# One kernel of windowed attention, layer norm, recurrent gates and a second norm: the softmax division moved into the layout of the values product, with two round trips through DRAM, new places for several transfers and new roles for the accumulator banks

## The reference

```
q, k, v = split(x @ w_in.T)                      # 16 heads of 16 features
scores = q . k / 4 + slope[head] * distance      # keys of the own and the previous block of 128
p = softmax(scores);  o = p @ v;  a = o @ w_out.T
x1 = layernorm(x + a)
for t in 16 sequences (the scan's first axis; c has one row for each of 512 tokens):
    f, i = sigmoid(x1[t] @ wf.T + c @ uf.T + bf), sigmoid(x1[t] @ wi.T + c @ ui.T + bi)
    g = tanh(x1[t] @ wc.T + c @ uc.T + bc);  c = f * c + i * g
h = tanh(x1 @ wo.T + c_final @ uo.T + bo)
out = layernorm(x1 + h)
```

## Time and profile before

| | |
|---|---|
| median of 3 runs | 994.1 us |
| the profiled execution: its own time, span of its instructions | 994.83 us, 992.7 us |
| PE busy | 911.2 us (92%), granted clock 0.955 on average |
| DVE busy | 714.1 us (72%) |
| ACT busy | 574.8 us (58%) |
| POOL busy | 409.0 us (41%) |
| DMA | 131.86 MB; the main queue's packets took 45.3% of 16 engines' span |

### The profile page before, as it was taken

The page is one execution under the profiler, slowest core; times in us unless marked ns, Lnnn a source line. Parts: engine busy times, 40 slices in busy tenths (PEclk is TensorE's granted clock), DMA queues, the critical chain, the costliest instruction groups (busy, mean ns, idle before and its releaser), DMA issues. The chain is left out here.

```text
span 992.7 us, 25986 instructions
## 1 busy us (share of the span) xinstructions
PE 911.2 (92%) x9500; PEld 749.7 (76%) x9500; DVE 714.1 (72%) x2795; ACT 574.8 (58%) x1167; POOL 409.0 (41%) x687
## 2 busy tenths in 40 slices
PE   3587889999999999999999999999999999989994
PEld 2365668888888888888888888888787876668884
DVE  7666677878787868787878787878787754337875
ACT  6044556565656565656565656565656554335786
POOL 6143343444535353535353535354444443001443
PEclk8586989999999999999999999999999989899998
DMA  7644454535454545353645454645444400131764
GB/s 265 164 124 127 131 139 132 151 122 156 124 151 128 145 134 150 123 154 125 153 128 151 128 143 137 149 131 147 133 121 138 119 23 22 44 106 46 215 204 131
DMA packets 93534, 131.86 MB, mean 133 GB/s; under 512 B 12128, under 2 KB 47584, under 8 KB 93408
## 3 DMA queue, kind: packets, MB, share of 16 engines
q1 hardware_dynamic: 93136, 129.95, 45.3%
q10 hardware_dynamic: 272, 0.26, 0.1%
HBM read 79.31 MB, written 50.33 MB: 131 GB/s over the span
## 5 line engine op out<-in xcount | busy, mean ns | idle before, releaser
L689 DVE CUSTOM_DVE_ANT_0 bank<-bank,mask 128x256 f32<-128x256 f32 (+1 forms) x1024 | 369.4, 423 | 130.7 <-PE bank L951 128.7
L448 ACT ACTIVATE Pt<-bank 128x512 f32<-128x512 f32 (+1 forms) x512 | 248.2, 536 | 193.4 <-PE bank L972 193.3
L347 POOL TENSOR_SCALAR_AFFINE_SELECT Pt<-Pt 128x512 f32<-128x512 f32 x256 | 170.4, 666 | 403.9 <-ACT Pt L448 403.9
L951 PE MATMUL bank<-Ks,Qs 59*128 59x256 f32 (+1 forms) x1024 | 148.2, 319 | 44.9 <-DVE max_q L689 31.3
L951 PEld LDWEIGHTS bank<-Ks,Qs 59*128 59x128 f32 x1024 | 107.3, 191 | 86.6 <-DVE max_q L689 42.5
L689 DVE DVE_READ_ACCUMULATOR2_ANT max_q<- 128x1 f32 x1024 | 144.9, 142 | 0.0
L349 POOL TENSOR_SCALAR_AFFINE_SELECT Pt<-Pt 128x384 f32<-128x384 f32 x256 | 144.7, 565 | 0.0
L986 PE MATMUL bank<-Pt,Vp 128*32 128x256 f32 (+1 forms) x2048 | 130.9, 377 | 0.0
L932 PE MATMUL bank<-x1T,Wg 64*128 64x512 f32 x960 | 127.9, 398 | 1.0 <-DVE o_tok L703 1.0
L932 PE MATMUL bank<-cT,Ug 64*128 64x512 f32 x960 | 125.7, 393 | 0.0
L972 PE MATMUL bank<-Qs,Ks 60*128 60x256 f32 (+1 forms) x1024 | 111.8, 271 | 0.7 <-ACT Pt L448 0.3
(11 more groups left out here) (111 smaller groups left out, 1354.7 us busy)
## 6 DMA issues: line engine op xcount, KB each, us to landing
parts_dram<-qk_parts SPq DMA_DIRECT2D x128, 256.0 KB
Qs<-parts_dram SPq DMA_DIRECT2D x128, 128.0 KB, 2.7
Ks<-parts_dram SPq DMA_DIRECT2D x128, 128.0 KB, 2.8
xt_raw<-in_xt SPq DMA_DIRECT2D x16, 512.0 KB, 4.5
Qs<-parts_dram SPq DMA_DIRECT2D x128, 64.0 KB, 2.7
Ks<-parts_dram SPq DMA_DIRECT2D x128, 64.0 KB, 2.7
x_res<-in_x SPq DMA_DIRECT2D x16, 512.0 KB, 3.9
x_dram<-y SPq DMA_DIRECT2D x16, 512.0 KB, 4.4
```

The source lines that it names most:

```text
L347: gp.affine_select(out=p4[:, :, 0:128], in_=p4[:, :, 0:128], compare_op=ALU.is_ge, fill=0.0, base=0, pattern=[[0, 4], [1, 128]], channel_m ...
L448: sc.activation(probabilities(g, 2 * pair + odd)[:, S * a:S * a + n], SC[odd][:, 0:n], ACT.Exp).then_inc(exp_done, 1)
L689: ins = ve.tensor_tensor_reduce(out=raw, in0=raw, in1=mask[:, keys], scale=1.0, scalar=MASKED, op0=ALU.add, op1=ALU.max, accum_out=max_q[: ...
L951: ins = te.matmul(MX[odd][:, 256 * (n % 2):256 * (n % 2) + 256][:, keys], Qs[rows, 2 * g + pair, n * WIN:(n + 1) * WIN], Ks[rows, 2 * g + ...
```

## The change

- In sequences 0 to 14 the division no longer goes through the token layout. After each `ctx_out` ACT waits for its own copy and sends `ctx_raw` to `ctx_dram` by a DMA from its own queue; the next `ctx_out` waits until that has landed. SP loads the 16 denominator rows into `den_q` (4 DMAs), DVE turns them (32 x 32 blocks), takes reciprocals and turns them back, SP stores them in `inv_dram` and loads them again spread over each head's 16 partitions (`inv_den`, 2 DMAs), and the contexts as `o_un` (2 DMAs). POOL multiplies the two, and ACT and DVE split `o_un` into `oT`. `ctx_transpose`, `normalise` and `o_transpose` are left for the last sequence only.
- SP: chunk 1's parts of sequence t go out in iteration t, behind the last maxima row of t - 1 and the refill of group 1, instead of at the end of iteration t - 1. The first maxima row goes ahead of the refill of group 2.
- The low part of the transposed input, `x_lo`, moves from DVE to POOL from sequence 2 on, and `x_hi` from slots 1 and 2 of the iteration before to slots 11 and 12 of the one before that.
- Banks: B0 is bank 4 and A1 bank 5 in each iteration, 6 and 7 take turns as A0 and B1. The transposes of the norm use A0 and B0, the first gates B1 and A1.
- `w_o` and `u_o` are loaded and split at the end of the attention stage, into the room of `w_in`.

```diff
+        ctx_dram = nc.dram_tensor("ctx_dram", [2, QUADS, 128, S], F32).ap()
+        inv_dram = nc.dram_tensor("inv_dram", [2, 32, S], F32).ap()
...
+            moving = PAIRS[1]
+            return (moving[t % 2], PAIRS[0][1]), (PAIRS[0][0], moving[1 - t % 2])
...
+            def load_denominators(t):
+
+                sp.wait_ge(den_cleared, 1)
+                for g in range(QUADS):
+                    wait(sp, ctx_stored[g], 16, t, 16)
+                wait(sp, inv_stored, 16, t - 1, 16)
+                rows = ctx_dram[t % 2].rearrange("g (h r) (q i) -> q (g h) r i", r=2 * D, i=128)[:, :, D, :]
+                for q in range(4):
+                    sp.dma_start(den_q[32 * q:32 * q + H, :], rows[q]).then_inc(den_in, 16)
+
+            def load_contexts(t, c):
+                for g in (2 * c, 2 * c + 1):
+                    wait(sp, ctx_stored[g], 16, t, 16)
+                wait(sp, otlo_done, 2, t - 1, c + 1)
+                rows = ctx_dram[t % 2, 2 * c:2 * c + 2].rearrange("g (h r) s -> (g h) r s", r=2 * D)[:, 0:D, :]
+                sp.dma_start(o_un[:, c, :], rows).then_inc(o_un_in[c], 16)
+
+            def store_inverses(t):
+                wait(sp, inv_turned, 1, t, 1)
+                sp.dma_start(inv_dram[t % 2].rearrange("r (q i) -> q r i", i=128), den_q[:, :]).then_inc(inv_stored, 16)
+
+            def spread_inverses(t):
+
+                wait(sp, inv_stored, 16, t, 16)
+                for c in range(KC):
+                    wait(sp, scaled_done, 2, t - 1, c + 1)
+                    rows = inv_dram[t % 2, 8 * c:8 * c + 8]
+                    sp.dma_start(inv_den[:, c, :], rows.unsqueeze(1).to_broadcast([8, D, S])).then_inc(inv_in[c], 16)
...
                 if p1: max_to_stack(t - 1, 3)
-                if now: stack(t, 1)
+                if now:
+                    stack(t, 1)
+                    if t: parts_to_dram(t, 1)
                 if p2:
                     wait(sp, y_done, 2, t - 3, 2)
                     sp.dma_start(x_res[:, :, :], x[t - 2].rearrange(tok, p=128)).then_inc(xres_in, 16)
+                if by_rows: load_contexts(t - 1, 0)
                 if real(t + 2): load_xt(t + 2)
                 if now:
+                    max_to_stack(t, 0)
                     stack(t, 2)
-                    max_to_stack(t, 0)
                     stack(t, 3)
                 if n1: parts_to_dram(t + 1, 0)
                 if now: max_to_stack(t, 1)
                 if p2:
                     wait(sp, x1_done, 4, t - 2, 4)
                     sp.dma_start(x1_dram[t - 2].rearrange(tok, p=128), y[:, :, :]).then_inc(x1_out, 16)
+                if by_rows: load_denominators(t - 1)
                 if n1: stack(t + 1, 0)
+                if by_rows: load_contexts(t - 1, 1)
                 if now: max_to_stack(t, 2)
-                if n1: parts_to_dram(t + 1, 1)
+                if by_rows:
+                    store_inverses(t - 1)
+                    spread_inverses(t - 1)
+                if t == B - 1: load_last_weights()
...
+            def x_lo(t, c):
+                wait(pool, xhi_done, 2, t, c + 1)
+                gp.tensor_tensor(xT[:, t % 2, 1, c, :], xt_raw[:, c, :], xT[:, t % 2, 0, c, :].bitcast(F32), ALU.subtract).then_inc(xlo_done, 1)
+
+            def scale_contexts(t, c):
+
+                wait(pool, o_un_in[c], 16, t, 16)
+                wait(pool, inv_in[c], 16, t, 16)
+                gp.tensor_tensor(o_un[:, c, :], o_un[:, c, :], inv_den[:, c, :], ALU.mult).then_inc(scaled_done, 1)
...
+                if p2 and t - 2 < B - 1:
+                    for c in range(KC):
+                        scale_contexts(t - 2, c)
...
+                    if real(t + 2):
+                        for c in range(KC):
+                            x_lo(t + 2, c)
...
-                wait(act, ct_ready, 4, t, g)
+                pt, pg = before(t, g)
+                if pt < B - 1:
+                    wait(act, ctx_stored[pg], 16, pt, 16)
+                else:
+                    act.wait_ge(ct_ready, g)
                 sc.activation(ctx_raw[:, :], bank[:, :], ACT.Copy).then_inc(ctx_done, 1)
-
-            def ot_hi(t, c, bank):
+                if t < B - 1:
+                    wait(act, ctx_done, 4, t, g + 1)
+                    sc.dma_start(ctx_dram[t % 2, g], ctx_raw[:, :]).then_inc(ctx_stored[g], 16)
+
+            def ot_hi(t, c):
                 if c == 0:
                     wait(act, op_ready, 2, t - 1, 2)
-                wait(act, ot_ready, 2, t, c + 1)
+                wait(act, scaled_done, 2, t, c + 1)
+                sc.activation(oT[:, 0, c, :], o_un[:, c, :], ACT.Copy).then_inc(othi_done, 1)
...
                 v_out(t, 0, A0)
+                if real(t + 2): x_hi(t + 2, 0)
                 attend(12)
                 v_out(t, 1, A1)
+                if real(t + 2): x_hi(t + 2, 1)
...
                 exps(t, 3, 3)
+                last_weights_hi()
                 c_hi(t - 2, 0)
                 c_hi(t - 2, 1)
                 layernorm(t - 1)
...
+            def turn_denominators(t):
+
+                wait(dve, den_in, 64, t, 64)
+                ve.transpose(den_t[:, :], den_q[:, :]).then_inc(den_turned, 1)
+
+            def invert_denominators(t):
+                wait(dve, den_turned, 1, t, 1)
+                own = den_t[:, :].rearrange("p (b r) -> p b r", r=32)[:, :, 0:H]
+                ve.reciprocal(own, own).then_inc(den_inverted, 1)
+
+            def turn_inverses(t):
+                wait(dve, den_inverted, 1, t, 1)
+                ve.transpose(den_q[:, :], den_t[:, :]).then_inc(inv_turned, 1)
+
+            def ot_lo(t, c):
+                wait(dve, othi_done, 2, t, c + 1)
+                minus_hi(oT[:, 1, c, :], o_un[:, c, :], oT[:, 0, c, :]).then_inc(otlo_done, 1)
...
                 attend(0)
-                if p1: normalise(t - 1, 0, A0)
+                if p3: forget(t - 3, 0)
+                attend(1)
+                if t == 0: x_lo(1, 0)
+                attend(2)
+                if t == 0: x_lo(1, 1)
                 if p2:
-                    ot_lo(t - 2, 0, B0)
-                    ot_lo(t - 2, 1, B1)
-                attend(1)
-                if n1: x_lo(t + 1, 0)
-                if p3: forget(t - 3, 0)
-                attend(2)
-                if n1: x_lo(t + 1, 1)
+                    ot_lo(t - 2, 0)
+                    ot_lo(t - 2, 1)
...
+                if p1: turn_denominators(t - 1)
                 if n1: qk_lo(t + 1, 3, B1)
-                if p1: normalise(t - 1, 3, A0)
-                if p2:
-                    x1_lo(t - 2, 0, B0)
-                    x1_lo(t - 2, 1, B1)
+                if p1: invert_denominators(t - 1)
+                if p2: x1_lo(t - 2, 0, A0)
+                if p1: turn_inverses(t - 1)
+                if p2: x1_lo(t - 2, 1, B0)
...
                 attend(0)
                 if p1:
-                    freed(pe, (x1lo_done, 2, t - 3, 1), (qklo_done, 4, t, 3))
-                    max_transpose(t - 1, 3, A0)
-                    freed(pe, (x1lo_done, 2, t - 3, 2), (qklo_done, 4, t, 4))
-                    values(t - 1, 1, A1)
-                    wait(pe, maxrow_done, 4, t - 1, 4)
-                    ctx_transpose(t - 1, 0, A0)
-                if p2:
-                    wait(pe, gate_done, 6, t - 3, 1)
-                    o_transpose(t - 2, 0, B0)
-                    freed(pe, (gate_done, 6, t - 3, 2), (ctx_done, 4, t - 1, 1))
-                    o_transpose(t - 2, 1, B1)
+                    freed(pe, (x1lo_done, 2, t - 3, 2), (qklo_done, 4, t, 3))
+                    max_transpose(t - 1, 3, B0)
+                    freed(pe, (x1lo_done, 2, t - 3, 1), (maxrow_done, 4, t - 1, 3))
+                    values(t - 1, 1, B1)
...
                     values(t - 1, 2, A1)
-                    wait(pe, maxrow_done, 4, t, 1)
-                    ctx_transpose(t - 1, 1, A0)
                 if n1:
...
                 values(t, 0, A1)
-                if p1:
+                if p2:
                     wait(pe, maxrow_done, 4, t, 3)
-                    ctx_transpose(t - 1, 3, A0)
-                if p2:
-                    freed(pe, (qklo_done, 4, t + 1, 3), (o_done, 4, t - 1, 3))
-                    x1_transpose(t - 2, 0, B0)
-                    freed(pe, (qklo_done, 4, t + 1, 4), (ctx_done, 4, t - 1, 4))
-                    x1_transpose(t - 2, 1, B1)
+                    x1_transpose(t - 2, 0, A0)
+                    freed(pe, (qklo_done, 4, t + 1, 3), (maxrow_done, 4, t, 2))
+                    x1_transpose(t - 2, 1, B0)

                 attend(14)
                 if p2:
-                    g0, g1 = gate_halves(0, A0, state_first=True), gate_halves(1, A1, state_first=True)
-                    wait(pe, o_done, 4, t - 1, 4)
+                    g0, g1 = gate_halves(0, B1, state_first=True), gate_halves(1, A1, state_first=True)
+                    freed(pe, (qklo_done, 4, t + 1, 4), (ctx_done, 4, t - 1, 4))
...```

```

(1 more changed line is left out.)

212 lines of the change are left out of this document (118 added, 94 removed).

## The result

| | before | after |
|---|---|---|
| median | 994.45 us (992.67 to 997.59, 4 runs) | 1051.52 us (1048.26 to 1054.38, 4 runs) |
| ratio | | 1.0569, 95% interval 1.0527 to 1.0611 |
| span of the profiled execution | 992.7 us | 1046.5 us |
| mean granted clock | 0.955 | 0.924 |
| DMA traffic | 131.9 MB | 164.8 MB |

A forecast was written before the change was run, and what follows sets the result against it. PE, busy 92% of the span, was taken as the bound. 14 x (-0.2 - 0.6 + 0) = -11, +4 late issues, -3 start, +1 end: -9 from 994.8, 985.8, put at 985 against the median; 8-in-10 range 957 to 1010.

The forecast's parts named there:

- What leaves PE: Transposes taken off PE in each iteration: 2.98 us, so PE reaches `project_qk` 1.89 us earlier, T + 15.7 from slot 0's start.
- Stretch A, the wait for `y`: Slots 0 to 5: PE waits 1.7 us before `project_qk` because `x_res` lands behind the parts; stretch total -0.2 us.
- the upper bound: Wait of 3 us before `project_qk` if ACT's store and the spreading of inverses start the parts' data a microsecond later.
- The split of a landing: The 3.9 us of an `x_res` load: 2.0 until data moves, 1.5 of data, 0.4 for confirmation.
- It decides from a wait of about 2 us: Wait of PE at `project_qk` from which the halved clock applies, 0.3 us more than the forecast's sum.
- rival 2: PE's wait at `project_qk` reaches 2 us or more and the clock falls in each iteration: 1012 us; chance 0.25.
- the 4 us of late issues: SP's issue of `x_res` late by 1.1 us in some 3.5 of 14 iterations, each moving PE's wait: +4 us.
- Stretch B: Slots 6 to 12: the third transpose leaves PE and `normalise` leaves DVE, maxima rows in time: -0.6 us an iteration.
- Stretch A, the output projection: Slots 0 to 5: `ot_lo` ready near T + 8, the projection asks at T + 9.6; costed at nothing.
- the cover: Spare 1.5 us before the output projection needs `ot_lo`; without it PE waits one for one.
- Stretch C: Slots 13 to 15: PE's saving is held back by `x1_lo` ending at 512.6: 0 us, bounds -0.5 and +0.5.

The follow-up runs named there:

- e3: The kernel before with only chunk 1's parts writes moved to where the changed kernel has them, ahead of `x_res`, no division by rows; 1037.0 us.
- e7: The changed kernel with the parts laid out in DRAM as 128 x 512 matrices, on all 16 engines, 12 refill transfers a quad for 8; 1016.1 us.
- e5: The changed kernel with the loads of xt and of the contexts' first half moved behind quad 1's maxima row; 1054.7 us.
- e1: The changed kernel with SP loading `x_res` ahead of the four writes of chunk 1's parts, not behind them; 1021.0 us.
- e4: The changed kernel with `x_res` ahead of chunk 1's parts, and loads of xt and the contexts' first half behind quad 1's maxima row; 1000.6 us.
- e6: The changed kernel with chunk 1's parts back at the end of SP's iteration, ahead of the store and spreading of the inverses; 1059.2 us.
- e13: e4 with the loads of contexts and inverses cut to one head of eight; 991.2 us.
- e14: The changed kernel with the loads of contexts and inverses cut to one head of eight; 1041.5 us.

## Why the prediction was wrong, point by point

- **What leaves PE** was right: slot 0 by 1.46 us where 1.47 was forecast, and PE at `project_qk` at T + 15.65 for T + 15.7.
- **Stretch A, the wait for `y`,** is the step that failed: its mechanism was right (DVE held by `x_res` behind the parts), its size was not. 1.7 us was forecast, within 0.1 to 3; measured are 49.4 us over 13, 3.8 in the mean and up to 5.6. The issue was right (T + 10.4 for T + 10.15); the term that was short is issue to landing, 6.5 in the sum and 7.6 in the median here (10.1 at most). e3 has 7.9 with the parts alone, without ACT's store and the spreading of inverses that I had named for the upper bound, and e7 has 5.2 with the parts on all engines. I had taken the parts at 184 GB/s, the rate of one row; at the 155 of e5's five stages 1.05 MB take 6.8 us and not 5.7, an estimate that covers the difference of the medians. The split of a landing (2.0 us until data moves, 1.5 of data, 0.4) no run shows.
- **"It decides from a wait of about 2 us"**, the point of rival 2, was right to within about a microsecond (see the last section), and so was its price of 1.6 us (4.61 - 3.02 = 1.6). With the wait past that point rival 2 was the case, with a chance of 0.25; it too had the wait short, 2.3 us, left out the 4 us of late issues, and so ended at 1012. That figure lay itself outside the range, which ended at 1010 though a quarter of the chances stood on it.
- **Stretch B** had the maxima rows in time with over a microsecond in hand. They cost 12.3 us, 8.1 of them in eight waits for quad 1's row. The sum counted SP's delay and not the bulk that a row stands behind; that this bulk is the cause is argued from e1 and e4, and no run isolates it in this kernel.
- **Stretch A, the output projection** was right: L1053 with `Wout` starts at T + 9.5, where T + 9.6 was forecast, with one wait of 0.6 us in the whole kernel. e6 shows what it costs when the cover is used up.
- **Stretch C** was right for the most part: no difference was forecast from the end of the values product to the next slot 0, 8.44 us before (508.82 to 517.26 in the earlier trace rows). Of nine iterations between 300 and 770 us five took 8.4 us, and four 8.7 to 9.9, three of these behind a maxima row that was 0.6 to 1.2 us late.

Put right, the sum comes out: 985, and 25.6 us more of waiting for `y` (49.4 less 14 x 1.7), less the 4 us for late issues that are in it now, 18.2 for the half clock, 12.3 for rows and 4.8 for refills: 1042, where the profiled execution took 1048.3; some 6 us are in none of these terms. The forecast's gain for PE was not wrong; it was paid back in one wait, which then cost its own half again in clock.

What stays open: which engines finish `x_res` last, and whether any order of SP's queue carries this division with a gain. The best of thirteen orders and layouts with the division by rows (e4) was level with the kernel before; e13, where part of the loads is left out, is only 0.5% faster than the kernel before, so the added loads aren't all that stands in the way.

## What to carry to other kernels

A DMA whose order is changed is paid for by what stands behind it: list the next four transfers of the queue with the time at which each is used, not the moved one alone, and put nothing that an engine waits for within 8 us behind a megabyte on half of the engines (7.2 to 7.9 us here). Where a sum puts PE's wait within a microsecond of the length at which the clock fell elsewhere in the trace, take the halved clock as the likeliest case and not as a tail. Before tuning an order, try the moved lines alone in the old kernel: here two lines showed 41 of the 57 us.

## What the runs showed that I had not expected

- **Waits and the clock.** In five kernels (after, e3, e5, e7, e14) 64 waits for `y` stand ahead of the same twelve matmuls. All 16 of 0.18 to 2.03 us left them at 3.0 us, 2.4 GHz. Of 18 between 2.06 and 3.07 us, 13 were followed by 4.4 to 5.5 us, and so were all 30 from 3.11 us on. So wait and price don't rise together: between 2 and 3.1 us the same wait is followed by either level. Nor is 2.03 us a limit: the wait ahead of the fall in the earlier trace rows was 1.98 us.
- **Issues take longer behind bulk.** SP's issue of `x_res` (columns: ns least, median, most):

```profile
L327 SPq DMA_DIRECT2D x_res<-in_x x16: 441/1237/1558, 132.0 to 900.9; - x16
```

  In e1, ahead of the parts, its median is 428 ns. Behind the parts one issue holds SP for 0.8 us more, and what stands behind it on SP is late by that too.
- **The number of transfers against their width.** One layout made the changed kernel 35 us faster, the kernel before 3 us faster and e4 25 us slower. Whether engines or SP's issues are scarce is a matter of the few microseconds ahead of each use, and the page's average share of SP's DMA queue (44 to 51% in all of these runs) says nothing on it.
